# Router logits with the padded router weights stationary in four column strips of the tensor engine, and one transpose to bring them back

## The chip, the core and the metric

The kernel runs on one core of a Trainium2 chip. The metric is the device time in microseconds (us) of one execution; a lower number is better. The engines of the core are named as the profile names them: PE is the tensor engine (PEld its weight loads), DVE the vector engine, ACT the scalar engine, POOL the GpSimd engine, and SP issues the DMAs.

## What is computed

Two transformer layers follow each other on an input of 4 batches of 512 tokens with 256 channels. The change touches the router of the first layer's mixture of experts:

```python
logits = x @ router_w.T                      # 8 experts, 256 channels
top_vals, top_idx = jax.lax.top_k(logits, 1)
scores = sigmoid(top_vals at top_idx, -inf elsewhere)
xr = x[None] * scores.T[:, :, None]
gate, up = split(einsum('eth,ehf->etf', xr, gate_up_proj))
routed_sum = einsum('etf,efh->eth', up * silu(gate), down_proj).sum(axis=0)
shared = (silu(x @ shared_gate_w) * (x @ shared_up_w)) @ shared_down_w
```

Here x is the layer-normalised output of the first attention. The kernel routes each token to its one expert, so the top index of all 2048 tokens decides which rows the expert tiles gather.

## The kernel before, in words

The first part of the kernel works through a list of steps (`a_steps`), the same list for every engine. Each engine walks it and does what is its own in each step. The list is written out by hand in the tables `A_START` to `A_END`. `attention_order` puts them between the attention steps: for each batch there are 16 slots, divided by `|`. In a slot PE does the scores of the next slot (`attS`, line 644), then the steps that the table names, then the probabilities times values of this slot (`attP`, line 658). A prefix says which batch a step belongs to: `-` the batch before, `+` the next, `=` two before, `.` the slot's own. `A_END` has no attention slots; its `-` means batch 3 and its `=` batch 2.

The steps that matter here, with batch b:

- `X`, `N`: transposes of the input and of the normalised rows. ACT copies them to `x_t` and `x1_t` (line 939).
- `rp`: the rotary embedding of batch b + 1 on DVE (lines 1119 to 1139). `T`: transposes of its result; ACT (line 923) and DVE (lines 1155 to 1159) split it into bf16 parts, and SP sends the parts to DRAM and back as stacks for the scores.
- `R`: the router logits (PE line 610 through `products`). For each of the 4 tiles of 128 tokens, the 128 x 128 block of `x1_t` is the stationary operand and 8 columns of `rw_t` move, for two halves of the channels: 8 products. DVE copies the 128 x 32 logits out (line 1175), takes the maximum (line 1178) and its index (line 1186), builds `onehot` (line 1189), and after ACT's exponential of the score (line 943) scales the rows (line 1198), which SP stores to DRAM.
- `Sg`, `Su`: the shared expert's gate and up products (line 610, 512 columns). ACT applies SiLU to Sg (line 950), DVE multiplies Su (line 1203). `D`: the shared down product (256 columns), which DVE adds (line 1208).
- `RK`: ranks of all tokens from `onehot` (PE), then a long chain on DVE (lines 1212 to 1264). `ID` (line 704): the token lists of the expert tiles; it waits for the one-hot tables that this chain makes (line 1256).
- `rw`: once, two transposes of the 8 x 256 router weights (line 602), copied to `rw_t` by DVE (line 1113).

All of these but the attention share three PSUM banks in rotation: `take` makes PE wait until the step that had the bank three steps before was consumed. A step more in the list turns the rotation by one.

Every product of float32 operands is issued as two PE records, each with a weight load, so the 8 products of R are 16 records. A transpose is one record.

After the list come the expert tiles (from line 714), then the second layer in the same style.

Of the kernel before, what the change touches and what calls it, by code (L numbers as in the profile page):

```python
# [29 lines left out]
P = 128  # L30
B = 4
# [10 lines left out]
E = 8  # L42
# [30 lines left out]
A_START = """X0 X1 Q0 Q1 Q2 Q3 rp0 rp1 +X0 +X1 V0 T0 rp2 T1 T2 +Q0 +Q1 +Q2 +Q3 +rp0 +rp1 +rp2"""  # L73
A_FIRST = """.rw0 | | | | | +T0 | >X0 | +T1 | +T2 | | >X1 | | | | | |"""
A_SECOND = """-F0 -F1 .V0 -G0 -F2 -F3 +Q0 | -G1 -P0 | -P1 +Q1 | +Q2 | +Q3 | +rp0 +rp1 +rp2 | -N0 -N1 | -R0 -Sg0 | -Sg1
-Sg2 -Sg3 | +T0 -Su0 | +T1 +T2 | -Su1 -Su2 | -Su3 | | -D0 | -D1 |"""
A_THIRD = """-F0 -F1 .V0 +X0 +X1 -G0 | -F2 -F3 +Q0 | -G1 -P0 | -P1 +Q1 | +Q2 | +Q3 +rp0 +rp1 +rp2 | -N0 -N1 | | -Sg0
-Sg1 -R0 -Sg2 -Sg3 | -Su0 | +T0 | +T1 +T2 -Su1 | -Su2 | -Su3 | -D0 | -D1 |"""
A_LAST = """.V0 -F0 -F1 | -G0 -F2 | | -F3 | -G1 -P0 -P1 | | -N0 | -N1 | -R0 | | | | | | | |"""
A_END = """-F0 -F1 =Sg0 -G0 -F2 -F3 =Sg1 -G1 -P0 =Sg2 =Sg3 =Su0 -P1 =Su1 =Su2 -N0 =Su3 =D0 -N1 -R0 =D1 RK0 -Sg0 -Sg1  # L80
-Sg2 -Sg3 -Su0 -Su1 ID0 -Su2 -Su3 -D0 -D1"""
# [69 lines left out]
def post_ln_layers(nc, ins, out):  # L151
# [4 lines left out]
    with ExitStack() as ctx:  # L156
# [60 lines left out]
        w_o = place([NC_, C])  # L217
        rw_t = place([NC_, E])
        s_gate = place([NC_, FE])
# [7 lines left out]
        h_t = place([NF, S])  # L227
        n_rw = place([C])
        ss = place([2, NT])
# [225 lines left out]
        def _(sp):  # L455
# [8 lines left out]
            for dst, src in ((w_o, ins["out_kernel"].rearrange("(c p) n -> p c n", p=P)), (tok_id, ins["tok_id"]),  # L464
                             (n_rw[0:E], ins["router_w"]), (iotae, ins["iotae"]), (iotaj, ins["iotaj"]),
                             (iotap, ins["iotap"])):
                sp.dma_start(dst, src).then_inc(s_small, 16)
# [128 lines left out]
        def _(pe):  # L596
# [20 lines left out]
            for step in a_steps:  # L617
                n, b, i = step
                if n == "rw":
                    pe.wait_ge(s_small, 96)  # L620
                    transposes(step, [(E * c, n_rw[0:E, cols(c)], ident[0:E, 0:E], P) for c in range(2)])
                elif n == "X":
                    pe.wait_ge(s_x[b], 16)
# [53 lines left out]
                elif n == "R":  # L677
                    consumed(pe, ("N", b, 0))
                    consumed(pe, ("N", b, 1))
                    products(step, [((P, E * t, E * (t + 1)), [(x1_of[b][:, c, cols(t)], rw_t[:, c, :]) for c in range(2)])  # L680
                                    for t in range(NT)])
                elif n in ("Sg", "Su"):
                    pe.wait_ge(s_w1, 48)
                    w = s_gate if n == "Sg" else s_up
                    products(step, [((P, 0, S), [(w[:, c, cols(i)], x1_of[b][:, c, :]) for c in range(2)])])
                elif n == "D":
                    for f in range(NF):
                        consumed(pe, ("Su", b, f))
                    products(step, [((P, C * t, C * (t + 1)), [(h_t[:, f, cols(2 * i + t)], s_down[:, f, :])
                                                              for f in range(NF)]) for t in range(2)])  # L690
                elif n == "RK":

                    consumed(pe, ("R", B - 1, 0))
                    pe.wait_ge(topped, 2 * B)
                    pe.wait_ge(s_const, 48)
                    pe.wait_ge(s_ones, 2)
                    flat = onehot.rearrange("p t e -> p (t e)")
                    products(step, [((P, 0, P), [(upper, flat)]), ((P, P, 2 * P), [(ones, flat)])])
                elif n == "ID":
                    dst = take(pe, step)  # L700
                    for t in range(TT):
                        if t % (TT // 2) == 0:
                            pe.wait_ge(hot_ready, t // (TT // 2) + 1)
                        last = nc.tensor.matmul(dst[:, 0:48], pos_hot[:, t, :], pick[:, t, :], start=(t == 0),
                                                stop=(t == TT - 1))
                    last.then_inc(full_of(step), 1)
# [196 lines left out]
        def _(act):  # L903
            copy = ACT.Copy
            for step in a_steps:
# [30 lines left out]
                elif n in ("X", "G", "N"):  # L936
# [3 lines left out]
                                         src, copy).then_inc(free_of(step), 1)  # L940
                elif n == "R":
                    act.wait_ge(topped, 2 * b + 1)
# [100 lines left out]
        def _(v):  # L1043
# [66 lines left out]
            for step in a_steps:  # L1110
                n, b, i = step
                if n == "rw":
                    nc.vector.tensor_copy(rw_t, filled(v, step)[:, 0:2 * E].rearrange("p (c e) -> p c e", c=2))\
                      .then_inc(free_of(step), 1)
                elif n == "rp":
                    if i == 0:
# [56 lines left out]
                elif n == "R":  # L1173
                    src = filled(v, step)[:, 0:NT * E].rearrange("p (t e) -> p t e", e=E)
                    nc.vector.tensor_copy(logits, src).then_inc(free_of(step), 1)
# [341 lines left out]
```

## Time and profile before

| what | value |
|---|---|
| median of 3 runs | 929.6 us (929.55, 929.6, 932.98) |
| profiled execution, its own time | 930.34 us |
| its span (first to last instruction) | 928.2 us |
| mean granted clock of PE | 0.943 of full speed |
| PE busy | 815.7 us, 88% |
| DVE busy | 455.8 us, 49% |
| ACT busy | 376.9 us, 41% |
| POOL busy | 97.5 us, 11% |

Times in the rows are us from the start of the span. In a timeline row the first number is the start, the second the busy time of a merged group, and x is the number of records in it. In square brackets stands the idle time of that engine just before, and what ended it.

### The profile page before, as it was taken

The numbers are of one execution on the slowest core, as the hardware profiler recorded it, in microseconds if no ns is written. First come the engines' busy times: TensorE is split into PE (matmuls) and PEld (weight loads), VectorE is DVE, ScalarE is ACT, GpSimd is POOL, SyncE is SP. The second block draws the span as 40 slices with busy tenths as digits, with TensorE's granted clock in tenths as the row PEclk, the third lists the DMA queues.
The fourth block names the chain that finished last, engine by engine and source line by source line (L and its number), as shares of the span: only waits on it lengthen the run. The fifth ranks groups of instructions, "written<-read, shape, count | busy, mean of one in ns | idle before, by whom it ended". The sixth has DMA issues, their size and how long they took to land. (4 is left out here: it accounts for less than half of the span.)

```text
span 928.2 us, 12127 instructions
## 1 busy us (share of the span) xinstructions
PE 815.7 (88%) x4099; PEld 439.0 (47%) x4100; DVE 455.8 (49%) x1321; ACT 376.9 (41%) x597; POOL 97.5 (11%) x111
## 2 busy tenths in 40 slices
PE   5498999999998989999997687978999979979986
PEld 3222434444435556666654334434454535533675
DVE  2722652563425712222245794777754764553263
ACT  3287775784761101111133113545332433156130
POOL 0000000000000011111631101231011101011000
PEclk9689999999999999999989698989899989999999
DMA  6467317016034151111114680004500180000000
GB/s 199 95 177 133 122 43 144 12 30 122 1 108 143 32 164 46 45 45 45 34 59 133 185 258 16 2 24 121 153 1 2 51 245 1 2 1 24 12 12 24
DMA packets 54848, 71.12 MB, mean 77 GB/s; under 512 B 8182, under 2 KB 49178, under 8 KB 53258
## 3 DMA queue, kind: packets, MB, share of 16 engines
q1 hardware_dynamic: 52924, 65.33, 25.9%
q0 software_dynamic: 1872, 5.11, 2.1%
q8 instruction: 31, 0.51, 0.2%
q14 instruction: 21, 0.17, 0.1%
HBM read 46.57 MB, written 23.72 MB: 76 GB/s over the span
## 5 line engine op out<-in xcount | busy, mean ns | idle before, releaser
L610 PE MATMUL ps<-arena 128*128 128x256 f32 (+5 forms) x1084 | 336.9, 460 | 17.7 <-DVE arena L1203 5.0
L610 PEld LDWEIGHTS ps<-arena 128*128 128x128 f32 (+1 forms) x1084 | 204.8, 199 | 108.4 <-issue 69.5
L931 ACT ACTIVATE arena<-ps 128x1024 f32<-128x1024 f32 x128 | 124.1, 1026 | 39.8 <-PE ps L644 39.6
L1369 DVE TENSOR_REDUCE arena<-ps 128x1 f32<-128x512 f32 (+3 forms) x176 | 101.2, 634 | 42.5 <-PE ps L834 41.7
L1023 ACT ACTIVATE arena<-ps 128x1024 f32<-128x1024 f32 (+3 forms) x128 | 83.2, 705 | 87.4 <-PE ps L856 87.2
L602 PE MATMUL ps<-arena 128*128 128x128 f32 (+4 forms) x429 | 68.6, 304 | 44.3 <-DVE arena L1090 17.7
L723 PE MATMUL ps<-arena 128*128 x184 | 88.0, 602 | 1.2 <-DVE arena L1274 1.2
L602 PEld LDWEIGHTS ps<-arena 128*128 128x128 f32 (+4 forms) x429 | 54.4, 154 | 66.2 <-DVE arena L1090 21.3
L644 PE MATMUL ps<-arena 96*128 96x512 bf16 x256 | 71.5, 392 | 12.4 <-DMA arena<-parts_dram 9.3
L832 PE MATMUL ps<-arena 96*128 96x128 bf16 (+3 forms) x256 | 65.0, 312 | 12.5 <-DVE arena L1369 6.7
L1458 POOL TENSOR_SCALAR_AFFINE_SELECT arena<-arena 128x512 f32<-128x512 f32 x64 | 42.2, 661 | 288.7 <-ACT arena L1023 288.5
L658 PE MATMUL ps<-arena 128*32 128x512 f32 x512 | 69.7, 612 | 0.0
L1417 POOL DMA_INDIRECT arena<-xs_dram,arena x23 | 21.9, 951 | 427.3 <-DVE arena L1268 321.0
L956 ACT ACTIVATE arena<-ps 128x512 f32<-128x512 f32 x23 | 13.7, 598 | 125.8 <-PE ps L723 125.8
L644 PEld LDWEIGHTS ps<-arena 96*128 96x128 bf16 x256 | 18.3, 98 | 87.9 <-ACT arena L931 36.1
L856 PE MATMUL ps<-arena 98*128 98x512 bf16 (+3 forms) x256 | 48.9, 310 | 11.9 <-ACT arena L1023 8.9
L869 PE MATMUL ps<-arena 128*32 128x128 f32 (+3 forms) x512 | 50.7, 468 | 0.0
L834 PE MATMUL ps<-arena 128*128 128x128 bf16 x256 | 50.4, 226 | 0.0
L832 PEld LDWEIGHTS ps<-arena 96*128 96x128 bf16 x256 | 25.5, 100 | 44.2 <-DVE arena L1369 27.9
L723 PEld LDWEIGHTS ps<-arena 128*128 128x128 f32 x184 | 33.7, 194 | 26.1 <-issue 25.0
L856 PEld LDWEIGHTS ps<-arena 98*128 98x128 bf16 x256 | 18.4, 99 | 57.0 <-issue 31.4
L740 PE MATMUL ps<-arena 128*128 x184 | 43.6, 380 | 0.8 <-ACT arena L962 0.8
(142 smaller groups left out, 701.5 us busy)
## 6 DMA issues: line engine op xcount, KB each, us to landing
arena<-stacks_dram SPq DMA_DIRECT2D x16, 768.0 KB, 6.4
arena<-in_gate_up_proj SPq DMA_DIRECT2D x8, 1024.0 KB, 9.7
arena<-parts_dram SPq DMA_DIRECT2D x48, 128.0 KB, 4.5
stacks_dram<-arena SPq DMA_DIRECT2D x16, 384.0 KB, 3.4
arena<-in_down_proj SPq DMA_DIRECT2D x8, 512.0 KB, 9.1
stacks_dram<-arena SPq DMA_DIRECT2D x16, 256.0 KB, 3.7
parts_dram<-arena SPq DMA_DIRECT2D x8, 384.0 KB, 4.3
yg_dram<-arena SPq DMA_DIRECT2D x23, 128.0 KB, 1.7
```

The lines of the kernel that those rows point to most:

```text
L602: last = nc.tensor.transpose(dst[0:rows, col:col + n], src, idn)
L610: last = nc.tensor.matmul(dst[0:rows, lo:hi], a, w, start=(n == 0), stop=(n == len(pairs) - 1))
L644: last = nc.tensor.matmul(ps[:, g, :], k_stack[0:STACK, b % 2, hg, cols(kt)], q_stack[0:STACK, b % 2, 4 * hg + g, :], start=True, stop=True)
L658: last = nc.tensor.matmul(ps[32 * g:32 * g + 32, 4, :], v_aug[:, kt, hg, :], (probs0, probs1)[i % 2][:, g, :], start=(kt == 0), stop=(kt = ...
L723: last = nc.tensor.matmul(ps[:, 2 * half + up, :], xg_t[:, half, c, :], gu[:, e, c, FE * up:FE * (up + 1)], start=(c == 0), stop=(c == 1))
L832: nc.tensor.matmul(dst[:, w * g:w * (g + 1)], cq_stack[0:STACK, b % 2, h0 + g, cols(qt)], ck_stack[0:STACK, b % 2, h0 + g, 0:w], start=Tru ...
L834: last = nc.tensor.matmul(dst[:, w * g + P * qt:w * (g + 1)], identb, negmask, start=False, stop=True, skip_group_check=True)
L856: last = nc.tensor.matmul(ps[:, g, P * kt:S], ck_stack[0:STACK + 2, b % 2, h, cols(kt)], cq_stack[0:STACK + 2, b % 2, h, P * kt:S], start= ...
L869: last = nc.tensor.matmul(ps[32 * g:32 * g + 32, 4, P * kt:S], cv_aug[:, b % 2, kt, 4 * hg + g, :], cprobs[:, i % 2, g, P * kt:S], start=( ...
L931: nc.scalar.activation(probs[:, 2 * p:2 * p + 2, :], ps[:, 2 * p:2 * p + 2, :], ACT.Exp)\
L1023: nc.scalar.activation(cprobs[:, i % 2, 2 * p:2 * p + 2, P * kt:S], ps[:, 2 * p:2 * p + 2, P * kt:S], ACT.Exp).then_inc(exp_done[p], 1)
L1369: nc.vector.tensor_reduce(mneg[:, qt, h0:h0 + nh], filled(v, step)[:, 0:nh * w].rearrange("p (h n) -> p h n", n=w), AX.X, ALU.max, negate= ...
```

## The change

The router weights come from the host as 256 x 32, the 8 experts padded with 24 zero columns, and are loaded straight into `rw_t` (128 partitions x 2 x 32), so `rw` with its two transposes and its copy goes. In R the roles are swapped: `rw_t` is stationary, 32 columns wide, and 128 tokens move. Token tile t writes to partitions 32t to 32t + 31 of the bank, which is column strip t of PE; the loop takes the channel half outside and the tile inside. DVE copies this 128 x 128 result to `lt`. A new step `RT` transposes it once on PE, after which the logits stand as before, with a stride of 32. The copy of the logits, the top-1 work and ACT's exponential belong to `RT` now. Three tables put `RT` behind `Sg` or `D` work; in `A_LAST` it has the next slot.

```diff
-A_FIRST = """.rw0 | | | | | +T0 | >X0 | ...
+A_FIRST = """| | | | | +T0 | >X0 | ...
 A_SECOND
-... | -N0 -N1 | -R0 -Sg0 | -Sg1
+... | -N0 -N1 | -R0 -Sg0 -RT0 | -Sg1
 A_THIRD
--Sg1 -R0 -Sg2 -Sg3 | -Su0 | ...
+-Sg1 -R0 -Sg2 -RT0 -Sg3 | -Su0 | ...
 A_LAST
-... | -N1 | -R0 | | ...
+... | -N1 | -R0 | -RT0 | ...
 A_END
-... -N1 -R0 =D1 RK0 -Sg0 -Sg1
+... -N1 -R0 =D1 -RT0 -Sg0 RK0 -Sg1
...
-        rw_t = place([NC_, E])
+        rw_t = place([NC_, 32])
+        lt = place([P])
...
-                             (n_rw[0:E], ins["router_w"]), ...
+                             (rw_t, ins["router_w"].rearrange("(c p) e -> p c e", p=P)), ...
...
                 elif n == "R":            # PE
                     consumed(pe, ("N", b, 0))
                     consumed(pe, ("N", b, 1))
-                    products(step, [((P, E * t, E * (t + 1)), [(x1_of[b][:, c, cols(t)], rw_t[:, c, :]) for c in range(2)])
-                                    for t in range(NT)])
+                    pe.wait_ge(s_small, 96)
+                    dst = take(pe, step)
+                    for c in range(2):
+                        for t in range(NT):
+                            last = nc.tensor.matmul(dst[32 * t:32 * t + 32, 0:P], rw_t[:, c, :], x1_of[b][:, c, cols(t)],
+                                                    start=(c == 0), stop=(c == 1))
+                    last.then_inc(full_of(step), 1)
+                elif n == "RT":
+                    consumed(pe, ("R", b, 0))
+                    transposes(step, [(0, lt, ident, P)])
...
                 elif n == "RK":           # PE
-                    consumed(pe, ("R", B - 1, 0))
+                    consumed(pe, ("RT", B - 1, 0))
...
-                elif n == "R":            # ACT
+                elif n == "RT":
                     act.wait_ge(topped, 2 * b + 1)
...
                 elif n == "R":            # DVE
-                    src = filled(v, step)[:, 0:NT * E].rearrange("p (t e) -> p t e", e=E)
+                    nc.vector.tensor_copy(lt, filled(v, step)[:, 0:P]).then_inc(free_of(step), 1)
+                elif n == "RT":
+                    src = filled(v, step)[:, 0:P].rearrange("p (t e) -> p t e", e=32)[:, :, 0:E]
                     nc.vector.tensor_copy(logits, src).then_inc(free_of(step), 1)
```

The change moves instructions at four places. Two of them are shown, the second of them on two engines. The first is PE where the router of batch 0 runs, inside the attention of batch 1 (`A_SECOND`). Rows of 32x512 are `attP`, 128x8 or 32x128 is R, 128x512 behind it is Sg0. Before:

```order
L610 MATMUL ps<-arena 128x8 [waits unit_free2,unit_free1,unit_free0]
L610 MATMUL ps<-arena 128x8 x7
L610 MATMUL ps<-arena 128x512 [waits unit_free0,shared_weights_loaded]
L610 MATMUL ps<-arena 128x512
L658 MATMUL ps<-arena 32x512 [waits exp_done0]
```

and changed:

```order
L682 MATMUL ps<-arena 32x128 [waits small_operands_loaded,unit_free1,unit_free0,unit_free2]
L682 MATMUL ps<-arena 32x128 x7
L611 MATMUL ps<-arena 128x512 [waits unit_free2,shared_weights_loaded]
L611 MATMUL ps<-arena 128x512
L603 MATMUL ps<-arena 128x128 [waits unit_free0,unit_free1]
L656 MATMUL ps<-arena 32x512 [waits exp_done0]
```

The transpose stands between Sg0 and attP, and waits for a bank that DVE frees by copying R's result.

The second place is DVE in `A_END`, from the router of batch 3 to the ranks. The 128x512 rows are the add of D (=D1) and, before it, of D0. Before:

```order
L1208 TENSOR_TENSOR arena<-ps,arena 128x512 [waits xs_ready,unit_full2]
L1175 COPY arena<-ps 128x32 [waits unit_full1]
L1178 MAX arena<-arena 128x8 [waits unit_free1]
...
L1189 TENSOR_TENSOR arena<-arena 128x32 [waits dve_chain]
L1193 TENSOR_SCALAR arena<-arena 128x4 [waits score_exp_ready]
L1194 RECIPROCAL arena<-arena 128x4 [waits dve_chain]
L1198 TENSOR_TENSOR arena<-arena 128x1024 [waits xs_in_dram,dve_chain]
L1208 TENSOR_TENSOR arena<-ps,arena 128x512 [waits xs_ready,unit_full2]
L1212 COPY arena<-ps 128x128 [waits unit_full0]
```

and changed:

```order
L1213 TENSOR_TENSOR arena<-ps,arena 128x512 [waits xs_ready,unit_full1]
L1177 COPY arena<-ps 128x128 [waits unit_full0]
L1213 TENSOR_TENSOR arena<-ps,arena 128x512 [waits xs_ready,unit_full1]
L1180 COPY arena<-ps 128x32 [waits unit_full2]
L1183 MAX arena<-arena 128x8 [waits unit_free2]
...
L1194 TENSOR_TENSOR arena<-arena 128x32 [waits dve_chain]
L1198 TENSOR_SCALAR arena<-arena 128x4 [waits score_exp_ready]
L1199 RECIPROCAL arena<-arena 128x4 [waits dve_chain]
L1203 TENSOR_TENSOR arena<-arena 128x1024 [waits xs_in_dram,dve_chain]
L1217 COPY arena<-ps 128x128 [waits unit_full1]
```

The top-1 work and the scaling of the rows stood ahead of D1's add; now they stand between that add and the copy of RK's counts.

The third is PE at the same place. Rows of 128x256 are D1, a pair of 128x128 RK, 128x512 Sg0. Before:

```order
L610 MATMUL ps<-arena 128x8 x7
L610 MATMUL ps<-arena 128x256 [waits unit_free1,unit_free2]
L610 MATMUL ps<-arena 128x256 x7
L610 MATMUL ps<-arena 128x128 [waits ones_ready,rope_tables_and_triangle_loaded,unit_free0,top_ready,unit_free1]
L610 MATMUL ps<-arena 128x128
L610 MATMUL ps<-arena 128x512 [waits unit_free1,shared_weights_loaded]
```

and changed:

```order
L682 MATMUL ps<-arena 32x128 x7
L611 MATMUL ps<-arena 128x256 [waits unit_free0,unit_free1]
L611 MATMUL ps<-arena 128x256 x7
L603 MATMUL ps<-arena 128x128 [waits unit_free2,unit_free0]
L611 MATMUL ps<-arena 128x512 [waits unit_free0,shared_weights_loaded]
L611 MATMUL ps<-arena 128x512
L611 MATMUL ps<-arena 128x128 [waits ones_ready,rope_tables_and_triangle_loaded,unit_free1,top_ready,unit_free2]
```

So RK, the last row, has moved behind the transpose and Sg0.

## Rows read from the trace of the kernel before

**Rows 1.** The page's busy times, PE.

```profile
PE 815.7 (88%) x4099; PEld 439.0 (47%) x4100; DVE 455.8 (49%) x1321; ACT 376.9 (41%) x597; POOL 97.5 (11%) x111
```
**Rows 2.** PE's waits from 4 to 346 us, and a timeline row.

```profile
PE ps L644 <- DMA arena<-parts_dram: 9.3, 3, 6.6
...
223.27 1.04 PE L644 MATMUL ps<-arena 96*128 96x512 bf16 x4 [1.62 <-DMA arena<-parts_dram]
```
**Rows 3.** Stretches: length, PE, PEld, DVE, ACT, POOL, clock, DMA, GB/s.

```profile
299.40:301.00 1.60, 0.87 (x7) 0.56 (x6) 0.69 (x1) 0.69 (x2) 0.00 (x0) 1.00 0.00 0
301.00:302.80 1.80, 1.80 (x17) 1.80 (x17) 0.00 (x0) 1.19 (x1) 0.00 (x0) 1.00 0.00 0
...
303.60:306.40 2.80, 2.80 (x9) 2.26 (x8) 2.48 (x13) 0.19 (x1) 0.00 (x0) 0.56 0.00 0
...
334.00:338.00 4.00, 3.38 (x6) 1.60 (x7) 0.42 (x1) 0.00 (x0) 0.94 (x1) 0.58 0.84 273
```
**Rows 4.** Timeline of PE at batch 2's router.

```profile
254.39 1.85 PE L610 MATMUL ps<-arena 128*128 128x8 f32 x16
256.17 1.07 PE L658 MATMUL ps<-arena 128*32 128x512 f32 x8
```
**Rows 5.** Timeline of PE, products in four column strips with 128 columns moving.

```profile
600.30 0.42 PE L869 MATMUL ps<-arena 128*32 128x128 f32 x8
600.66 0.82 PE L856 MATMUL ps<-arena 98*128 98x384 bf16 x4
```
**Rows 6.** Timeline of PE, a group of transposes.

```profile
112.52 1.04 PE L602 MATMUL ps<-arena 128*128 128x128 f32 x8
```
**Rows 7.** Timeline of PE, the step rw.

```profile
48.38 0.38 PE L602 MATMUL ps<-arena 8*128 8x8 f32 x2
```
**Rows 8.** Timeline of all engines at batch 0's router.

```profile
115.15 2.19 PEld L610 LDWEIGHTS ps<-arena 128*128 128x128 f32 x18
...
115.36 3.67 PE L610 MATMUL ps<-arena 128*128 128x8 f32 x20
...
118.96 1.06 PE L658 MATMUL ps<-arena 128*32 128x512 f32 x8
...
120.20 0.19 DVE L1175 COPY arena<-ps 128x32 f32<-128x32 f32 x1
```
**Rows 9.** Timeline, PE and ACT after it.

```profile
128.74 0.60 PE L602 MATMUL ps<-arena 128*64 128x128 f32 x4 [0.63 <-ACT arena L950]
...
132.88 0.61 PE L644 MATMUL ps<-arena 96*128 96x512 bf16 x2 [0.16 <-ACT arena L931]
...
130.89 1.94 ACT L931 ACTIVATE arena<-ps 128x1024 f32<-128x1024 f32 x2
```
**Rows 10.** Timeline, PE and ACT after batch 1's router.

```profile
197.15 1.06 PE L658 MATMUL ps<-arena 128*32 128x512 f32 x8
...
198.83 1.28 ACT L931 ACT_TABLE_LOAD   x1 [0.98 <-PE ps L644]
```
**Rows 11.** Timeline of A_END, PE and DVE.

```profile
300.99 17.91 PE L610 MATMUL ps<-arena 128*128 128x8 f32 x60 [0.73 <-ACT arena L939]
302.95 0.19 DVE L1175 COPY arena<-ps 128x32 f32<-128x32 f32 x1 [2.40 <-PE ps L610]
...
304.99 1.23 DVE L1198 TENSOR_TENSOR arena<-arena 128x1024 f32<-128x1024 f32 x1
...
308.19 0.69 DVE L1208 TENSOR_TENSOR arena<-ps,arena 128x512 f32<-128x512 f32 x1 [1.98 <-PE ps L610]
...
308.80 0.28 DVE L1212 COPY arena<-ps 128x128 f32<-128x128 f32 x1
...
316.28 2.36 DVE L1256 TENSOR_TENSOR arena<-arena 128x1024 bf16<-128x1024 f32 x2
...
318.74 0.56 PE L704 MATMUL ps<-arena 128*128 128x48 bf16 x16
...
320.46 3.67 PE L610 MATMUL ps<-arena 128*128 128x512 f32 x8 [1.16 <-DVE arena L1203]
```

More of the change, by code:

```diff
@@ L73 @@
 A_START = """X0 X1 Q0 Q1 Q2 Q3 rp0 rp1 +X0 +X1 V0 T0 rp2 T1 T2 +Q0 +Q1 +Q2 +Q3 +rp0 +rp1 +rp2"""
-A_FIRST = """.rw0 | | | | | +T0 | >X0 | +T1 | +T2 | | >X1 | | | | | |"""
-A_SECOND = """-F0 -F1 .V0 -G0 -F2 -F3 +Q0 | -G1 -P0 | -P1 +Q1 | +Q2 | +Q3 | +rp0 +rp1 +rp2 | -N0 -N1 | -R0 -Sg0 | -Sg1
+A_FIRST = """| | | | | +T0 | >X0 | +T1 | +T2 | | >X1 | | | | | |"""
+A_SECOND = """-F0 -F1 .V0 -G0 -F2 -F3 +Q0 | -G1 -P0 | -P1 +Q1 | +Q2 | +Q3 | +rp0 +rp1 +rp2 | -N0 -N1 | -R0 -Sg0 -RT0 | -Sg1
 -Sg2 -Sg3 | +T0 -Su0 | +T1 +T2 | -Su1 -Su2 | -Su3 | | -D0 | -D1 |"""
 A_THIRD = """-F0 -F1 .V0 +X0 +X1 -G0 | -F2 -F3 +Q0 | -G1 -P0 | -P1 +Q1 | +Q2 | +Q3 +rp0 +rp1 +rp2 | -N0 -N1 | | -Sg0
--Sg1 -R0 -Sg2 -Sg3 | -Su0 | +T0 | +T1 +T2 -Su1 | -Su2 | -Su3 | -D0 | -D1 |"""
-A_LAST = """.V0 -F0 -F1 | -G0 -F2 | | -F3 | -G1 -P0 -P1 | | -N0 | -N1 | -R0 | | | | | | | |"""
-A_END = """-F0 -F1 =Sg0 -G0 -F2 -F3 =Sg1 -G1 -P0 =Sg2 =Sg3 =Su0 -P1 =Su1 =Su2 -N0 =Su3 =D0 -N1 -R0 =D1 RK0 -Sg0 -Sg1
+-Sg1 -R0 -Sg2 -RT0 -Sg3 | -Su0 | +T0 | +T1 +T2 -Su1 | -Su2 | -Su3 | -D0 | -D1 |"""
+A_LAST = """.V0 -F0 -F1 | -G0 -F2 | | -F3 | -G1 -P0 -P1 | | -N0 | -N1 | -R0 | -RT0 | | | | | | |"""
+A_END = """-F0 -F1 =Sg0 -G0 -F2 -F3 =Sg1 -G1 -P0 =Sg2 =Sg3 =Su0 -P1 =Su1 =Su2 -N0 =Su3 =D0 -N1 -R0 =D1 -RT0 -Sg0 RK0 -Sg1
 -Sg2 -Sg3 -Su0 -Su1 ID0 -Su2 -Su3 -D0 -D1"""
@@ L227, in post_ln_layers @@
         h_t = place([NF, S])
-        n_rw = place([C])
+        place([C - P - NC_ * (32 - E)])
         ss = place([2, NT])
@@ L464, in _ @@
             for dst, src in ((w_o, ins["out_kernel"].rearrange("(c p) n -> p c n", p=P)), (tok_id, ins["tok_id"]),
-                             (n_rw[0:E], ins["router_w"]), (iotae, ins["iotae"]), (iotaj, ins["iotaj"]),
+                             (rw_t, ins["router_w"].rearrange("(c p) e -> p c e", p=P)), (iotae, ins["iotae"]), (iotaj, ins["iotaj"]),
                              (iotap, ins["iotap"])):
@@ L618, in _ @@
                 n, b, i = step
[L619 to L622, printed above, removed]
+                if n == "X":
                     pe.wait_ge(s_x[b], 16)
@@ L1111, in _ @@
                 n, b, i = step
[L1112 to L1115, printed above, removed]
+                if n == "rp":
                     if i == 0:
@@ L1512 @@
         arrays[name] = w
+    router = np.zeros((C, 32), np.float32)
+    router[:, 0:E] = arrays["router_w"].T
+    arrays["router_w"] = router
     arrays.update(shape_constants())
```

## The prediction

> **What bounds the kernel.** I read the page's busy times first. PE is busy 88% of the span [rows 1], far ahead of DVE and ACT, so time taken from PE is worth something unless another wait stands beside it. Second, PE's waits in the first 346 us, where all of the change lies. Between 60 and 300 us PE hardly pauses. The waits that a shift could vanish into are three for stacks from DRAM, the largest at the start of the attention of batch 0, and one of 1.62 us at 223.27 [rows 2]. Third, the timeline at the four routers. In the slots PE and ACT run nearly level, so what PE gains can end in a wait for ACT. Fourth, the end of the list, where two chains meet: PE's shared products and DVE's ranks both reach ID at 318.7 (DVE's one-hot tables end at 316.28 + 2.36 = 318.64, and ID starts at 318.74), and the next gate or up product waits for DVE until 320.46 [rows 11]. There DVE sets the time. From there on the expert tiles and layer two follow at fixed distance, so a shift of that product is a shift of the end.
>
> Fifth, the clock. Behind batch 3's router the granted clock falls to 0.56, that is half speed (1.2 of 2.4 GHz) in most of the stretch [rows 3]. What PE did before it fell: transposes, a pause, and R with 8 moving columns. It falls again at 334 us, after the pause before the first expert tile.
>
> **R itself.** It is 16 records in 254.39 to 256.17, so 1.78 us [rows 4], and weight loads come every 0.12 us (18 in 2.19 [rows 8]): loading 128 columns of weights sets its pace, not the 8 columns that move. The new form has a near relative in layer two: 8 records, four strips, 128 columns, from 600.30 until the next kind of product starts at 600.66, 0.36 us [rows 5]. R is twice that number. The tail and the change of array form are paid once: 0.42 us for the group less about 0.2 us of passing through leaves 0.21 for 8 records, so 16 records take 0.36 + 0.21 = 0.57, and I add 0.1 for entering the strips: 0.67. The gain is 1.8 - 0.67 = 1.15 us per batch. Bounds: 2 x 0.42 = 0.84 (gain 0.95), and 0.43 where attP follows in the same strips (gain 1.3).
>
> The Trainium skill ("TensorEngine Tiling (Array Packing)", Instruction Overhead) speaks against this: each matmul has an overhead of some 60 cycles, so a moving side of 1 costs what 60 costs, and a tiling factor should not be taken from a dimension that is already small. Sixty cycles at the full clock are an estimate of 25 ns a record, 0.4 us for the old R, and the swap would gain nothing: the sum below would be 3.5 us higher. The 0.12 us a record that the rows show disagree, and I go by them.
>
> **RT itself.** One transpose is 1.04 / 8 = 0.13 us on PE [rows 6]. The copy to `lt` is 128 x 128 out of PSUM, 0.28 us like the copy at 308.80 [rows 11]. Neither matters alone; where they stand does.
>
> **rw gone.** It took 0.3 us of PE (two small transposes, 0.38 us [rows 7]). PE's next waits for stacks take such a gain: 0, with -0.4 as the bound if that cover fails. The load of the router weights in 256 pieces of 128 bytes is still 32 KB among the early loads, and its first reader is now at 115 us: 0.
>
> **Batch 0's router.** R starts at 115.36, and with Sg0 now ends near 117.8. RT needs `lt`, and DVE is busy with the rotary work of batch 2 until it reaches the logits copy at 120.20 [rows 8]. So PE waits: copy 0.28, handing over 0.1, transpose 0.13, change of form 0.1, and attP starts at 120.85 instead of 118.96: +1.9 us. Part comes back. At 128.74 PE waited 0.63 for ACT's SiLU, and ACT's next exponential came only at 130.89, with PE waiting for it at 132.88 [rows 9]. ACT now does Sg0's SiLU before the router's exponential, so it is not late by these 1.9: its order then gives 130.8 for that exponential by the same durations. PE therefore passes on about 0.45 to 1.1 from there. I take +0.6; bounds 0 and +1.9.
>
> **Batch 1's router.** The table puts Sg2 between R and RT, and DVE is free when R ends. PE gains 1.15 - 0.13 = 1.0, and attP at 197.15 comes forward. But ACT now loads the exponential's table, does the score, and loads SiLU's again between Sg2 and Sg3; the load at 198.83 [rows 10] comes only some 0.3 earlier. I take -0.6; bounds -1.0 and -0.2.
>
> **Batch 2's router.** R stands before attP, in the same strips, so nothing is paid for leaving; RT is in the next slot, where DVE is idle. -1.25 + 0.2 for the transpose and its change of form: -1.0; bounds -1.3 and -0.7. This is behind the wait at 223.27, so it can't vanish there; what the two before leave passes through that wait mostly, since its stacks come from transposes that shift too.
>
> **Batch 3's router, in A_END.** Four terms.
> - R: -1.15.
> - The clock. D1's 16 records start at 302.8 and last until about 308. At full speed they take 3.45 (as at 320.46, where 8 records of twice the width took 3.67). So half speed costs 1.75 us. With R keeping the array's strips full and D1 starting 1.15 sooner, I expect the clock to hold: -1.75; bounds -1.75 and 0.
> - DVE's order. Before, the top-1 work and the scaling ran from 302.95 to 304.99 + 1.23 = 306.22, 3.27 us, hidden under D1. Now they come behind D1's add and ahead of the rank chain: that chain starts 3.27 us later after D1's end. RT itself hides under the add (0.61 us). RK waits for `onehot`, some 2.3 us after that add starts, with Sg0 as cover. On DVE nothing covers: +3.3; bounds +3.0 and +3.6.
> - The clock again. PE runs out of work: after RK five units of about 1.75 end near 11.3 us after D1's end, ID can go on at 13.8, and the next product at 15.5 (320.46 - 308.19 + 3.27). That is 4 us with little but ID in it, longer than the pauses before the falls of [rows 3], so the clock is likely to fall, and the shared products behind it run at half speed until it rises: +0.9, bounds 0 and +1.75.
>
> **Sum.** 0 + 0.6 - 0.6 - 1.0 - 1.15 - 1.75 + 3.3 + 0.9 = +0.3 us. The profiled execution took 930.34, 928.2 of it span, so it gives 930.6 for its like. Two of the three runs shown and the median stand 0.7 lower, at 929.6; for the median I forecast 929.9. A measurement here can tell about 0.5% from no change, 4.6 us, so this is no change.
>
> **Rivals.**
> 1. The copy out of PSUM becomes the bound: DVE's place in the queue holds PE each time. Batch 0's wait passes whole (+1.9), batches 1 and 2 gain nothing because ACT paces them, and A_END gives -1.15 + 3.3 and the later fall whole +1.75, with the clock in D1 restored or not (-1.75 or 0). That is +4.0 to +5.8: 933.6 to 935.4. For: DVE is late by 2.4 us at 120.20, and the order of A_END. Against: ACT was the late one at 128 to 133. It decides if PE's first scores after batch 0's router are still over 1.5 us late at 135 us. The Trainium skill ("TensorEngine Tiling (Array Packing)", PSUM Bottleneck) says that tiling speeds up TensorE and not the evacuation, so the PSUM copy may become the bottleneck.
> 2. The swap gains nothing, because the strips do not run side by side. A record of 512 columns takes 3.67 / 8 = 0.46 us [rows 11], one of 128 a quarter of it, and 16 in a row 1.8 us, as before. Then 3.4 us are missing at batches 1 to 3, and the time is 933.3. Against: 8 such records took 0.42 [rows 5]. The Trainium skill's rule on the 60 cycles (same page as above, Instruction Overhead) would come to the same time.
> 3. Only PE's time counts: all four R gains (4.6) and the clock (1.75), and the rank chain is hidden after all. 923.6. Against: ID started right at DVE's end.
> 4. The clock is kind: no fall behind the pause, and batch 0's wait vanishes whole. 0 - 0.8 - 1.0 - 1.15 - 1.75 + 3.3 = -1.4: 928.2.
> 5. The clock falls in D1 as before, and again later: 929.9 + 1.75 = 931.7.
>
> **Chances.** Forecast 0.59 (own range 928.9 to 931.2), rival 1 0.15, rival 2 0.03, rival 3 0.04, rival 4 0.11, rival 5 0.08. Slower by over 0.5% is above 934.25: half of rival 1 and a little of 2, 0.09. Faster by over 0.5% is rival 3, 0.04. Within 0.5%: 0.87. The range, 928.0 to 934.0, leaves out rival 3, the upper half of rival 1 and little else.
>
> **What would show it.** R's 16 records in 0.6 to 0.85 us; at batch 0 a wait of PE of 2 to 3 us before the transpose, for DVE; `attP` near 120.8; at batch 2 a gain of about 1 us that ACT keeps; the granted clock at 1.0 in D1 of A_END; the counts' copy 3.9 us after D1's add starts instead of 0.6; a pause of PE of about 2.5 us before ID, with the clock at half speed after it. The forecast is wrong if the first expert tile starts more than 2 us from 334.3, if R's records are spaced by 0.1 us, or if ID does not wait.

## The result and the profile after

The median is 931.13 us for the changed kernel and 928.96 us for the kernel before, over 22 runs of each on one chip: a ratio of 1.0032, with a 95% interval of 1.0019 to 1.0046. (The ratios here are estimates over all runs of a session, and differ a little from the quotient of the two medians, 1.0023 for this pair.) In a second session an unchanged copy of the changed kernel had 930.37 against 929.36 and a ratio of 0.9999 (0.9981 to 1.0017). By the bound of 0.5% that is no change; the first session shows it slightly slower, clear of the noise, the second does not. 931.13 lies inside the forecast range. The profiled execution took 930.71 us, 928.6 of it span, with a mean granted clock of 0.940.

The page's busy times after:

```profile
PE 809.5 (87%) x4101; PEld 431.7 (46%) x4102; DVE 457.2 (49%) x1324; ACT 377.2 (41%) x597; POOL 98.2 (11%) x111
```

PE is 6.2 us less busy than in [rows 1], and nothing of that reaches the end. PE's waits from 4 to 346 us say where some of it went:

```profile
PE ps L642 <- DMA arena<-parts_dram: 9.7, 3, 7.6
...
PE ps L603 <- DVE arena L1177: 2.5, 1, 2.5
...
PE ps L710 <- DVE arena L1261: 1.6, 2, 1.0
```

The first line answers to [rows 2] and hardly differs. The two below it are new: the transpose `RT` waits for DVE's copy of R's result (L1177), and the token lists (L710) wait for DVE's one-hot tables.

**R itself.** The timeline of PE at batch 2's router, first the record group ahead of [rows 4] in the kernel before, then the kernel after:

```profile
253.52 1.04 PE L644 MATMUL ps<-arena 96*128 96x512 bf16 x4
```

```profile
253.45 1.04 PE L642 MATMUL ps<-arena 96*128 96x512 bf16 x4
254.42 0.64 PE L682 MATMUL ps<-arena 128*32 128x128 f32 x16
254.88 1.04 PE L656 MATMUL ps<-arena 128*32 128x512 f32 x8
```

From the start of R to the start of attP it is 0.46 us here, where attP follows in the same strips, against 1.78 before. Ahead of a full-array product it is 0.57 (the rows of batch 0, next). R starts 0.97 us after the scores that stand ahead of it, against 0.87 before (254.42 - 253.45 and 254.39 - 253.52), so going from the full array into the strips costs 0.10 us.

**Batch 0's router.** Timeline of PE, then a stretch of the same time (length; PE, PEld, DVE, ACT, POOL busy; the granted clock; DMA share; GB/s):

```profile
114.63 0.65 PE L682 MATMUL ps<-arena 128*32 128x128 f32 x16
115.20 1.98 PE L611 MATMUL ps<-arena 128*128 128x512 f32 x4
119.72 0.33 PE L603 MATMUL ps<-arena 128*128 128x128 f32 x1 [2.54 <-DVE arena L1177]
119.98 1.87 PE L656 MATMUL ps<-arena 128*32 128x512 f32 x8
```

```profile
120.00:122.00 2.00, 2.00 (x10) 0.27 (x10) 1.69 (x16) 0.31 (x2) 0.00 (x0) 0.53 0.01 4
```

PE waits 2.54 us, and after it the granted clock falls to about half, so attP takes 1.87 us instead of the 1.06 of [rows 8]. In the trace of before the clock stayed at 1.00 there.

**A_END.** Timeline of PE, then of DVE, then stretches, beside [rows 11] and [rows 3]:

```profile
299.67 0.65 PE L682 MATMUL ps<-arena 128*32 128x128 f32 x16 [0.73 <-ACT arena L945]
300.25 3.72 PE L611 MATMUL ps<-arena 128*128 128x256 f32 x16
303.81 0.27 PE L603 MATMUL ps<-arena 128*128 128x128 f32 x1
...
316.64 0.36 PE L710 MATMUL ps<-arena 128*128 128x48 bf16 x8 [0.96 <-DVE arena L1261]
317.69 0.37 PE L710 MATMUL ps<-arena 128*128 128x48 bf16 x8 [0.69 <-DVE arena L1261]
319.45 6.38 PE L611 MATMUL ps<-arena 128*128 128x512 f32 x8 [1.39 <-DVE arena L1208]
```

```profile
304.00 0.69 DVE L1213 TENSOR_TENSOR arena<-ps,arena 128x512 f32<-128x512 f32 x1 [3.34 <-PE ps L611]
304.61 0.18 DVE L1180 COPY arena<-ps 128x32 f32<-128x32 f32 x1
...
306.64 1.23 DVE L1203 TENSOR_TENSOR arena<-arena 128x1024 f32<-128x1024 f32 x1
307.78 0.28 DVE L1217 COPY arena<-ps 128x128 f32<-128x128 f32 x1
```

```profile
301.00:303.80 2.80, 2.80 (x14) 2.42 (x13) 0.00 (x0) 0.00 (x0) 0.00 (x0) 1.00 0.00 0
...
318.00:321.00 3.00, 1.61 (x5) 0.84 (x3) 2.11 (x7) 0.00 (x0) 0.51 (x1) 0.51 0.00 0
```

D1's 16 records run at the full clock, in 3.56 us (300.25 to 303.81). The counts' copy starts 3.78 us after D1's add (304.00 to 307.78), where it was 0.61 before. PE pauses around the token lists, and the eight shared records behind them take 6.38 us at half speed, against 3.67 in [rows 11].

**Where the time went.** The list cuts well into stretches between fixed instructions, and most of these agree to 0.02 us over all traces in which the clock held. The table has their lengths, from the starts of a group of attP (counted from 0 through the list), of the counts' copy (L1212 of before, L1217 after) and of the first transpose of the first expert tile. All columns but "before" and "after" belong to the experiments below. The last row is the rest of the span.

| stretch | before | before_again | after | after_again | b0_fill | fill_pause | end_rt_first | b0_rt_later | both_moves | before_late_router |
|---|---|---|---|---|---|---|---|---|---|---|
| batch 0's router: attP 16 to 26 | 41.97 | 41.96 | 43.78 | 43.61 | 42.13 | 42.14 | 42.14 | 40.17 | 40.18 | 41.96 |
| batch 1's: 26 to 46 | 85.86 | 85.87 | 85.46 | 85.46 | 85.47 | 85.46 | 85.46 | 85.47 | 85.47 | 85.87 |
| stacks from DRAM: 46 to 47 | 7.11 | 6.68 | 6.45 | 6.10 | 6.61 | 6.48 | 6.55 | 6.09 | 6.51 | 6.81 |
| batch 2's: 47 to 63 | 42.11 | 42.11 | 40.87 | 40.87 | 40.88 | 40.88 | 40.87 | 40.87 | 40.88 | 42.12 |
| A_END: 63 to counts' copy | 39.00 | 37.31 | 39.29 | 39.30 | 39.30 | 39.29 | 36.78 | 39.30 | 36.79 | 38.81 |
| counts' copy to first expert tile | 25.20 | 25.21 | 27.91 | 27.98 | 25.36 | 25.21 | 25.24 | 26.94 | 25.23 | 26.59 |
| start of the first expert tile | 334.00 | 331.42 | 335.69 | 334.73 | 331.39 | 331.66 | 328.84 | 329.76 | 326.08 | 333.63 |
| from there to the end | 594.2 | 595.3 | 593.0 | 594.1 | 596.2 | 597.1 | 596.1 | 596.9 | 593.0 | 596.3 |

From before to after, in the profiled pair, that is +1.81 at batch 0, -0.40 at batch 1, -0.66 at the stacks, -1.24 at batch 2, +0.29 in A_END and +2.71 behind it; attP 16 itself starts 0.82 earlier. The sum is +1.69, and 1.2 us of it are gone by the end of the span. Part of that is that before has half speed in its first expert products [rows 3] and after the full clock. Which of these belongs to the change, and which to one execution, is what the experiments had to tell. The last row bounds what a single trace can tell of the whole: the same instructions behind the list take 593.0 to 597.1 us in these traces, a scatter larger than most of the effects ahead of it. So the stretches up to the first expert tile show the mechanism, and the medians show what the whole time makes of it.

### The profile page after: what moved, and what is told of

Read it like the earlier page. It is cut to its first block and busy times, and to the rows that moved or that the text cites. A ratio compares the mean times of both kernels' runs of the same rounds, so it can differ in the third digit from the quotient of the medians.

```text
span 928.6 us, 12141 instructions
## 1 busy us (share of the span) xinstructions
PE 809.5 (87%) x4101; PEld 431.7 (46%) x4102; DVE 457.2 (49%) x1324; ACT 377.2 (41%) x597; POOL 98.2 (11%) x111
## 5 line engine op out<-in xcount | busy, mean ns | idle before, releaser
L611 PE MATMUL ps<-arena 128*128 128x256 f32 (+3 forms) x1020 | 327.9, 470 | 18.8 <-DVE arena L1208 5.2
L611 PEld LDWEIGHTS ps<-arena 128*128 128x128 f32 (+1 forms) x1020 | 195.4, 198 | 109.1 <-issue 72.1
L603 PE MATMUL ps<-arena 128*128 128x128 f32 (+2 forms) x431 | 70.3, 307 | 45.4 <-DVE arena L1096 17.6
L603 PEld LDWEIGHTS ps<-arena 128*128 128x128 f32 (+2 forms) x431 | 55.5, 155 | 67.2 <-DVE arena L1096 21.2
L746 PE MATMUL ps<-arena 128*128 x184 | 43.6, 380 | 0.8 <-ACT arena L968 0.8
```

The source lines that it names most:

```text
L603: last = nc.tensor.transpose(dst[0:rows, col:col + n], src, idn)
L611: last = nc.tensor.matmul(dst[0:rows, lo:hi], a, w, start=(n == 0), stop=(n == len(pairs) - 1))
```

## The experiments

Two theories of the end stood first: that the order of A_END costs what R gives, or that the clock does. Later the question became what the two new pauses do to the clock. Expectations speak of theories A and B; each names its own.

The medians of before were 928.96 in the session of after, 929.63 in that of end_rt_first, b0_rt_later and both_moves, 929.36 in that of after_again, the two fills and before_late_router, and 927.43 in the last.

| kernel | median us | runs | ratio to before | 95% interval |
|---|---|---|---|---|
| after | 931.13 | 22 | 1.0032 | 1.0019 to 1.0046 |
| after_again | 930.37 | 12 | 0.9999 | 0.9981 to 1.0017 |
| end_rt_first | 927.86 | 12 | 0.9979 | 0.9954 to 1.0003 |
| b0_rt_later | 926.59 | 12 | 0.9974 | 0.9949 to 1.0000 |
| both_moves | 921.92 | 12 | 0.9929 | 0.9904 to 0.9955 |
| b0_fill | 929.63 | 12 | 0.9997 | 0.9982 to 1.0011 |
| fill_pause | 928.75 | 12 | 0.9987 | 0.9971 to 1.0004 |
| before_late_router | 932.64 | 12 | 1.0034 | 1.0016 to 1.0051 |
| three_moves | 923.25 | 10 | 0.9952 | 0.9931 to 0.9974 |
| both_again | 922.70 | 12 | 0.9940 | 0.9921 to 0.9959 |

### The kernel before, once more (before_again)

An unchanged copy, executed once, to see whether the half speed in D1 belongs to the program.

> The kernel before once more, for its clock alone. Theory A (the old R with 8 moving columns and the pause before it let the clock fall, and the change cures that): the granted clock is again near 0.5 in D1 behind batch 3's router, and D1's add starts over 7 us after R's start. Theory B (a fall there is a matter of how the execution lies against the clock's own beat): in this execution D1 runs at 1.0 and its add starts about 5.5 us after R's start, or the fall lies elsewhere.

It took 928.78 us, span 926.7. Timeline of its PE, and one stretch with the clock:

```profile
300.08 16.23 PE L610 MATMUL ps<-arena 128*128 128x8 f32 x60 [0.73 <-ACT arena L939]
...
317.88 3.67 PE L610 MATMUL ps<-arena 128*128 128x512 f32 x8 [1.17 <-DVE arena L1203]
```

```profile
304.00:308.00 4.00, 4.00 (x18) 2.62 (x17) 3.54 (x13) 1.52 (x2) 0.00 (x0) 1.00 0.39 131
```

The same 60 records that took 17.91 us in [rows 11] take 16.23, because the clock is 1.00 throughout. So theory A fails as it stands: the fall of [rows 3] came in that execution and not in this one, and the old R does not bring it about by necessity. Theory B's reason for it, how an execution lies against the clock, is not shown by these two traces. Nor is it shown whether the new R makes the fall rarer: D1 ran at the full clock in all nine traces with the new R and in two of three with the old. A_END takes 37.31 us in this trace, and the change makes it 1.98 longer, not 0.29.

### RT ahead of D1 in A_END (end_rt_first)

```diff
-... -R0 =D1 -RT0 -Sg0 RK0 -Sg1
+... -R0 -RT0 =D1 RK0 -Sg0 -Sg1
```

> The changed kernel with RT put before D1 in the end's table, so that the top-1 work hides under D1 again; PE waits about 0.6 us for DVE's copy ahead of RT. Theory A (the place of RT in the end costs 3.3 us of DVE's chain and then a pause with a fall of the clock): the copy of the counts comes 5.7 us after R's start instead of 8.1, PE has no pause over 0.5 us before ID, no fall of the clock at 318 to 325 us, and the time is 2.5 to 5 us under the changed kernel, so 926 to 928.6, ratio to before 0.997 to 1.000. Theory B (the transpose and the copies themselves, or batch 0's wait, cost the time): within 1 us of the changed kernel, 930 to 932.

Timeline of PE, then of DVE:

```profile
298.01 0.64 PE L682 MATMUL ps<-arena 128*32 128x128 f32 x16 [0.73 <-ACT arena L945]
299.06 0.33 PE L603 MATMUL ps<-arena 128*128 128x128 f32 x1 [0.41 <-DVE arena L1177]
299.27 14.44 PE L611 MATMUL ps<-arena 128*128 128x256 f32 x44
313.54 0.56 PE L710 MATMUL ps<-arena 128*128 128x48 bf16 x16
315.27 3.67 PE L611 MATMUL ps<-arena 128*128 128x512 f32 x8 [1.17 <-DVE arena L1208]
```

```profile
301.46 1.23 DVE L1203 TENSOR_TENSOR arena<-arena 128x1024 f32<-128x1024 f32 x1
303.00 0.69 DVE L1213 TENSOR_TENSOR arena<-ps,arena 128x512 f32<-128x512 f32 x1 [0.31 <-PE ps L611]
303.60 0.28 DVE L1217 COPY arena<-ps 128x128 f32<-128x128 f32 x1
```

PE pays 0.41 us of waiting for the copy, and DVE does the top-1 work and the scaling while D1 runs, ending before D1 does. The counts' copy comes 5.59 us after R's start instead of 8.11 (299.67 to 307.78). A_END is 2.51 us shorter than after, and the pauses before the token lists are gone, with the clock at 1.00 to the end of the list. Theory A holds, and the median lies in its range: the order on DVE took back what R gave, and more. The clock did fall in this trace too, but behind the list, in the first expert products.

### RT one slot later at batch 0 (b0_rt_later)

```diff
-... | -N0 -N1 | -R0 -Sg0 -RT0 | -Sg1
+... | -N0 -N1 | -R0 -Sg0 | -RT0 -Sg1
```

> The changed kernel with batch 0's RT one slot later, so that PE does not wait 2.5 us for DVE behind the rotary work. Theory A (that wait vanishes in the wait for stacks near 223 us): attP of batch 1's last slots comes 1 us earlier near 187 us, the wait for stacks near 223 us grows, and the total stays within 0.5 us of the changed kernel. Theory B (it passes to the end): 1 to 1.5 us less.

Batch 0's stretch is 40.17 us, 1.97 shorter than in the traces where the clock held behind PE's wait (42.14), and 3.6 shorter than after's. Nothing of it vanishes on the way: batch 1's stretch stays 85.47, and the wait for the stacks doesn't grow (6.09 us between attP 46 and 47, the shortest of all). So my theory A, under which the wait for the stacks takes the gain, fell, and B holds in kind; its 1 to 1.5 us were too low. The kernel is 0.26% below before, with an interval that reaches 1.0000. The pause before the token lists is still there, and the clock fell behind it in this trace too (26.94 us).

### Both (both_moves, both_again)

Both edits above in one kernel, run in two sessions.

> Both moves. Theory A: as end_rt_first alone within 0.5 us, 926 to 928.6. Theory B: the two add up, so 1 to 1.5 us less than end_rt_first.

> Both moves once more beside it. Theory A (the gain of about 0.7 per cent over before is real and comes from the two places): ratio to before 0.991 to 0.995, no wait of PE over 0.7 us behind batch 0's router, no pause ahead of ID, and the clock at 1.0 at both. Theory B (the first timing was a lucky one): ratio 0.996 to 0.999.

Timeline of PE at batch 0, and in A_END, of both_moves:

```profile
118.82 0.33 PE L603 MATMUL ps<-arena 128*128 128x128 f32 x1 [0.58 <-DVE arena L1177]
...
310.78 0.57 PE L710 MATMUL ps<-arena 128*128 128x48 bf16 x16
312.51 3.67 PE L611 MATMUL ps<-arena 128*128 128x512 f32 x8 [1.16 <-DVE arena L1208]
```

The two stretches are 40.18 and 36.79 us: each move does beside the other exactly what it did alone. PE's wait behind batch 0's router is 0.58 instead of 2.54, the clock holds, and the first expert tile starts at 326.08, 9.6 us ahead of after. In both sessions the kernel beats the one before, by 0.7% (0.45 to 0.96) and 0.6% (0.41 to 0.79), which is theory A of both_again. This is the version to keep. The median is 5.9 us under that of end_rt_first in the same session, far more than the 1 to 1.5 us of theory B of both_moves. Batch 0's stretch gives 2.0 of it; 3.1 more stand, in the two traces, behind the list, where these kernels have the same instructions. Whether the second move has a part in that isn't shown.

### The changed kernel, once more (after_again)

> The changed kernel once more, beside the three below. Theory A (the two waits of PE, 2.5 us behind batch 0's router and about 2 us ahead of ID, cost their length and at times a fall of the clock): the waits are there again with the same length, the clock may or may not fall behind each, and the time is 930 to 932. Theory B (the fall of the clock at these places is fixed): it falls at 120 us and at 318 us as before.

Timeline of PE at batch 0's router, and a stretch behind it:

```profile
119.21 0.47 PE L603 MATMUL ps<-arena 128*128 128x128 f32 x1 [2.54 <-DVE arena L1177]
119.61 1.94 PE L656 MATMUL ps<-arena 128*32 128x512 f32 x8
```

```profile
120.00:122.00 2.00, 2.00 (x10) 0.24 (x3) 1.76 (x17) 0.59 (x2) 0.00 (x0) 0.50 0.01 4
```

The clock falls at both places again, and the stretches are 43.61 and 27.98 us. But in end_rt_first and fill_pause the same wait of 2.5 us at batch 0 was followed by the full clock. So the falls follow these pauses often, not always.

### PE kept busy in the wait at batch 0 (b0_fill), and in the pause before the token lists (fill_pause)

The first computes Sg0 of batch 0 twice, the second Su1 of batch 3, each into the same place:

```diff
-products(step, [((P, 0, S), [...])])
+times = 2 if step == ("Sg", 0, 0) else 1
+products(step, [((P, 0, S), [...])] * times)
```

(in fill_pause the step is `("Su", B - 1, 1)`).

> The changed kernel with batch 0's Sg0 computed twice, 4 more records of 0.43 us in PE's wait for DVE behind batch 0's router; the output is unchanged. Theory A (the wait itself costs about 1.5 us, a fall of the clock up to 1.8 more in some executions): the wait shrinks from 2.5 to 0.8 us, the clock stays at 1.0 there, attP starts when it did, and the median is 0 to 1 us under the changed kernel. Theory B (falls of the clock make up most of the cost): 1.5 us or more under it. Theory C (PE's time is what counts): 1.7 us over it.

> The changed kernel with batch 3's Su1 computed twice, 4 more records in PE's pause ahead of ID; the output is unchanged. Theory A (DVE's chain sets the time and the pause lets the clock fall): ID comes when it did, PE's pause ahead of it shrinks to under 0.5 us, the clock stays up at the shared products behind it, and the median is 1 to 2.5 us under the changed kernel, 929 to 930. Theory B (the clock's part is small): within 0.7 us of the changed kernel. Theory C: 1.7 us over it.

Timeline of PE of b0_fill at batch 0:

```profile
114.92 3.70 PE L611 MATMUL ps<-arena 128*128 128x512 f32 x8
119.43 0.33 PE L603 MATMUL ps<-arena 128*128 128x128 f32 x1 [0.82 <-DVE arena L1178]
119.69 1.06 PE L656 MATMUL ps<-arena 128*32 128x512 f32 x8
```

and of fill_pause before the token lists, with the clock:

```profile
305.09 10.98 PE L611 MATMUL ps<-arena 128*128 128x128 f32 x28 [0.62 <-issue]
315.91 0.82 PE L711 MATMUL ps<-arena 128*128 128x48 bf16 x16
318.12 3.67 PE L611 MATMUL ps<-arena 128*128 128x512 f32 x8 [1.40 <-DVE arena L1209]
```

```profile
318.00:321.00 3.00, 2.88 (x7) 1.44 (x8) 1.53 (x4) 0.00 (x0) 1.53 (x2) 1.00 0.03 7
```

In b0_fill the extra 1.72 us of products hide wholly in the wait, attP runs in 1.06 us, and the stretch is 42.13 instead of the 43.6 to 43.8 of the traces with a fall. In fill_pause the pauses of 0.96 and 0.69 are filled, the shared product takes 3.67 instead of 6.38, and the last stretch is 25.21, as before. Both traces are as theory A has them. Each is of one execution, though, and neither shows that the filling kept the clock up. The clock held without it too: at batch 0 in end_rt_first and in fill_pause, whose wait there was not filled (120.00 and 120.26 below), with the same stretch (42.14), and before the token lists in b0_fill, whose pause there was not filled (25.36). Against after_again in the same session the medians are 0.7 and 1.6 us lower, with intervals that overlap; the falls' share of the median is not measured. Theory C, that PE's extra 1.7 us count, fell in both. PE of fill_pause at batch 0:

```profile
120.00 0.33 PE L603 MATMUL ps<-arena 128*128 128x128 f32 x1 [2.54 <-DVE arena L1178]
120.26 1.06 PE L656 MATMUL ps<-arena 128*32 128x512 f32 x8
```

### The old R with the new order on DVE (before_late_router)

The kernel before, with R behind D1, so that the top-1 work stands where the change has it:

```diff
-... -N1 -R0 =D1 RK0 -Sg0 -Sg1
+... -N1 =D1 -R0 -Sg0 RK0 -Sg1
```

> The kernel before with the end's table in the order D1, R, Sg0, RK, so the old router with its top-1 work behind D1's add, and nothing else of the change. Theory A (the order of DVE's work in the end is the dear part): the copy of the counts comes about 3 us later after batch 3's N1 than before, plus R's own 1.8 us which now is behind D1 too in the chain to the logits, a pause of PE ahead of ID appears, and the time is 3 to 5 us over before, ratio 1.003 to 1.005. Theory B (the extra copy and transpose are the dear part): less than 1 us over before.

Timeline of PE:

```profile
315.90 0.36 PE L704 MATMUL ps<-arena 128*128 128x48 bf16 x8 [0.96 <-DVE arena L1256]
316.95 0.37 PE L704 MATMUL ps<-arena 128*128 128x48 bf16 x8 [0.69 <-DVE arena L1256]
318.71 5.06 PE L610 MATMUL ps<-arena 128*128 128x512 f32 x8 [1.39 <-DVE arena L1203]
```

The same pauses of 0.96 and 0.69 us appear with the old R, the product behind them is slow here too (5.06 us), A_END is 1.50 us longer than in before_again, and the kernel is 0.34% slower than before. Theory A holds: the loss at the end belongs to the order, and it needs neither the strips nor the transpose. In size, A_END's loss of 1.50 us is half of the 3 us that I expected for it. From the first product behind N1 to the counts' copy it takes 2.4 us longer (307.04 - 298.52 against 306.21 - 300.08), but 0.9 us come back, because D1 starts right behind N1's transposes, where R waited 0.73 us for ACT's copy.

### A third move, at batch 1 (three_moves)

Beside both moves, RT of batch 1 goes one slot later:

```diff
--Sg1 -R0 -Sg2 -RT0 -Sg3 | -Su0 | ...
+-Sg1 -R0 -Sg2 -Sg3 | -RT0 -Su0 | ...
```

> Both moves, and batch 1's RT one slot later, so that ACT does the four SiLU of batch 1 under two table loads fewer between them. Theory A (batch 1's router gained 0.4 us instead of 1.0 because ACT's table loads stood between Sg2 and Sg3): the stretch from the attP of batch 1's third-last shared slot to the stack wait is 0.4 to 0.7 us shorter than in both_moves, and the time is at or just under both_moves, 920.5 to 922. Theory B (it was not ACT): no difference in that stretch.

Timelines of ACT behind batch 1's router, of both_moves first and then of three_moves:

```profile
193.15 1.28 ACT L956 ACT_TABLE_LOAD   x1
194.45 0.60 ACT L956 ACTIVATE arena<-ps 128x512 f32<-128x512 f32 x1
195.06 1.28 ACT L937 ACT_TABLE_LOAD   x1
```

```profile
193.15 0.60 ACT L956 ACTIVATE arena<-ps 128x512 f32<-128x512 f32 x1 [1.12 <-PE ps L611]
194.73 1.28 ACT L937 ACT_TABLE_LOAD   x1 [0.98 <-PE ps L642]
```

The exponential of the score no longer stands between two SiLUs. It runs at 197.84 under the table that the attention's exponentials have loaded, and two table loads of 1.28 us go, the one ahead of it (L949) and the one behind it (L956). Batch 1's stretch falls from 85.47 to 84.96 us. The stretch behind it, attP 46 to 47 with its wait for the stacks from DRAM, is 6.76 us against 6.51 in both_moves and 6.34 in both_again; that it takes the gain back is possible and not shown, since this stretch differs by as much between two executions of one kernel (7.11 and 6.68 us in before and before_again). The medians are 923.25 and 922.70, so no gain is measured; a third move isn't worth keeping.

## Why the prediction was right, and where it failed

The forecast was no change at 929.9, and the kernel measured no change at 931.13, though the terms make up that sum in another way. The base of the forecast, 929.6 from three runs, also stood 0.6 us above the median of the 22. By its steps, first what the forecast gave, then what the table shows between traces in which the clock held. The rows of rw and of the stacks are differences of means, over the three traces with the old R and the nine with the new one:

| term | forecast | measured, clock held | with a fall |
|---|---|---|---|
| rw gone | 0 (-0.4) | about -0.7, not resolved | |
| batch 0's router | +0.6 | +0.17 | +1.8 |
| batch 1's | -0.6 | -0.40 | |
| stacks from DRAM | 0 | about -0.4, not resolved | |
| batch 2's | -1.0 | -1.24 | |
| A_END: R and DVE's order | -1.15 + 3.3 | +1.98 | |
| A_END: clock in D1 restored | -1.75 | 0 | |
| pause before the token lists | +0.9 | +0.15 | +2.7 |
| sum | +0.3 | about -0.4 | up to +3.8 |

- **R itself.** Forecast 0.67 us, with 0.1 of it for entering the strips. Measured: 0.57 from R's start and 0.10 ahead of it, so 0.67, and 0.11 less where attP follows in the strips. The strips do run side by side; sixteen records one behind the other would have taken 1.8 us. That the loads of 128 columns set the old pace fits the rows, which have a load every 0.12 us [rows 8]; no run separates it from the other things that the swap changed. Rival 2 fell. The Trainium skill ("TensorEngine Tiling (Array Packing)", Instruction Overhead) has some 60 cycles for each matmul; by that both forms would cost an estimated 0.4 us. The new form agrees: its 16th record starts 0.37 us after the first (0.64 busy, less 0.27 for one record), 25 ns a record. The old one, at 1.78 us or 0.11 us a record, does not. So the verdict that the swap gains nothing, which the prediction worked out from that rule and the page itself does not state, was wrong for this case.
- **rw.** The first attP starts between 47.1 and 48.7 us in all kernels, in no order that follows the change. attP 16 starts at 92.75, 92.28 and 91.47 in the three traces with rw, and at 90.92 to 92.20 in the others. The gain is inside that scatter. The load of the weights is not still 32 KB, as the prediction has it, but grows from 8 x 256 to 256 x 32 float32, 8 to 32 KB; no run shows a cost of that.
- **Batch 0.** The wait of 2 to 3 us came (2.54), and attP follows R's start by 5.35 us instead of 3.60 (forecast 5.49). PE's waits of 0.63, 0.16 and 0.23 us that followed in the kernel before (128 to 134 us) are gone, and by attP 26 only +0.17 is left, so +0.6 was too much; that the clock might fall behind this wait wasn't in the sum. And b0_rt_later shows that the forecast had the wrong yardstick: the stretch could have been 1.8 us *shorter* than before.
- **Batches 1 and 2** came out within 0.25 us. Batch 1 keeps only 0.40 because the exponential with its table loads comes later, between Sg2 and Sg3; three_moves, without it there, has 0.51 more.
- **The order on DVE.** Forecast +3.3 us, measured 3.78 - 0.61 = 3.17. With R's 1.21 off, that leaves 1.96 of the 1.98 that A_END shows. It is the largest term. end_rt_first takes it off again (2.51 us, not all 3.17, since PE waits 0.41 for the copy and transposes ahead of D1), and before_late_router shows it with the old R.
- **The step that failed** is "I expect the clock to hold: -1.75", the clock term in D1. The clock did hold in D1, as the sign list had it, but before_again shows that it holds there before the change as well. In the profiled pair the term came, 1.69 us (39.00 against 37.31). But a fall seen in one profiled execution was booked as a cost that every execution of the old kernel has. How many of the 22 executions behind the median had it isn't known, so the gain for the median is open, between 0 and those 1.7 us.
- **The clock behind the pause** was foreseen in kind and under-sized: 0.9 was half of its bound of 1.75, and a fall costs 1.2 to 2.6 (26.59 to 27.98 in the table's last stretch against 25.36), since half speed can last through the next eight records (6.38 against 3.67). The pause itself was not one of 2.5 us ahead of ID, as forecast, but 0.96 and 0.69 us, ahead of and within the token lists.
- **Behind the list** the prediction has everything follow at fixed distance. The last row of the first table shows 593.0 to 597.1 us there instead, for the same instructions, so a shift of the first expert tile reaches the end only to within a few us in one execution.
- **Rival 5**, no credit for D1 and a later fall, 931.7, lies nearer to the 931.13 than the forecast's 929.9. Its later fall was there; its fall in D1 was not in any trace of the changed kernel. Rival 4's condition, no fall behind the pauses, was not met in either trace of the changed kernel. Rivals 1 and 3 lie outside what was measured (rival 3's own terms give 923.3, not 923.6).

So the sum was right by errors that cancel. Where the clock holds, the missing -1.75 is made up by terms that were too high: 0.75 for the pause, 0.7 for rw, 0.4 each for batch 0 and the stacks, 0.2 each for batch 2 and A_END (batch 1 goes 0.2 the other way). That is luck and not a check of the terms. The medians are apart by +2.2 us in one session and +1.0 in the other (by the ratios +3.0 and -0.1), between the sum without falls, -0.4, and the sum with both, +3.8. Rival 1's condition, first scores of PE over 1.5 us late at 135 us, is not met: even behind the fall, attP 26, at 135 us, starts 0.99 us late in the profiled pair, and where the clock held it starts at 133.8 to 134.3 us, against 133.4 to 134.7 with the old R. The copy of L1177 is itself only 0.29 us. It is the copy's place in DVE's queue that cost time. The Trainium skill (same page, PSUM Bottleneck) says that evacuation may become the bottleneck when matmuls get faster; the traces agree in the place and not in the kind, since not the amount evacuated but the order of the queue decided.

Open: what decides whether a fall comes in a given execution, and how often each comes in the median. No run here made the falls come or stay away at will with the pauses left in.

## What to carry to other kernels

When a step becomes two with a handover between engines, give the second half its place by the consumer's queue and not by the producer's: here batch 0's stretch was 2.0 us longer with the transpose in one place than one slot later, and 3.6 where the clock fell too, and A_END was 2.5 us longer with it behind a large product than ahead of it. Before booking a stretch at half speed as a cost of the kernel, look at a second profiled execution of the same kernel. And a fall of the clock behind a wait of PE can cost as much again: 1.5 to 1.6 us behind the 2.54 us here, 1.2 to 2.6 behind the 0.96 and 0.69. So moving the wait away can be worth more than its length. That filling it with extra products does the same is not shown.

## What the runs showed of the hardware

- The granted clock is not a property of the program alone, and in single executions the instructions behind the list, the same in all kernels here, took 593.0 to 597.1 us. The kernel before fell to 0.56 in D1 in one execution and kept 1.00 in the next; the wait of 2.54 us at batch 0 was followed by half speed (1.2 of 2.4 GHz) in two traces and by full speed in two. The pauses of 0.96 and 0.69 us around small bf16 products were followed by a fall in four traces of five.
- A fall costs 1.5 to 1.6 us behind the wait at batch 0 (43.61 and 43.78 against 42.14), 1.2 to 2.6 us behind the pauses at the token lists, and 1.7 us in D1 (39.00 against 37.31).
- Products with 128 x 32 stationary and 128 columns moving, in four column strips, ran at 29 ns a float32 record (0.46 us for 16, with 25 ns between starts inside the group), where the same work with 128 x 128 stationary and 8 columns moving took 0.11 us a record. Entering the strips cost 0.10 us (0.97 against 0.87 from the scores ahead to R), leaving them 0.11 (0.57 against 0.46).
